# Attention and expert kernel: other PSUM banks for the second group's scores, finer last weight loads, two masks taken over by ScalarE and GpSimd

## What is computed

```python
q, k = exp(x @ Wq.T + bq), exp(x @ Wk.T + bk)        # per head, 16 heads of 8
v = x @ Wv.T + bv
kv = cumsum(k[..., None] * v[..., None, :], axis=1)   # over the tokens
den = sum(q * cumsum(k, axis=1), -1)
x1 = layernorm(x + (einsum(q, kv) / den) @ Wo.T + bo)
scores = sigmoid(x1 @ gate_w.T)                       # 32 experts, 2 of 4 groups, then top 8
w = 2.5 * chosen scores / their sum
moe = sum_e w_e * (silu(x1 @ gate_e.T) * (x1 @ up_e.T)) @ down_e.T  + the same, unweighted, of the shared expert
out = layernorm(x1 + moe)
```

## Time and profile before

| | us |
|---|---|
| median of 3 runs | 457.80 (457.75 to 458.01) |
| the profiled execution | 457.99 |
| its span (first to last instruction) | 456.2 |
| PE busy | 425.7 (93%) |
| DVE busy | 345.7 (76%) |
| POOL busy | 290.6 (64%) |
| ACT busy | 275.8 (60%) |
| DMA, mean | 99 GB/s |

### The profile page before, as it was taken

The page is one execution under the profiler, slowest core; times in us unless marked ns, Lnnn a source line. Parts: engine busy times, 40 slices in busy tenths (PEclk is TensorE's granted clock), DMA queues, the critical chain, the costliest instruction groups (busy, mean ns, idle before and its releaser), DMA issues.

```text
span 456.2 us, 10923 instructions
## 1 busy us (share of the span) xinstructions
PE 425.7 (93%) x4004; PEld 327.3 (72%) x4004; DVE 345.7 (76%) x912; ACT 275.8 (60%) x536; POOL 290.6 (64%) x217
## 2 busy tenths in 40 slices
PE   5888999999999999999999999999999999798992
PEld 3656787768776887868777787868877787476771
DVE  2648777896979877896968967796968968767653
ACT  3746357763696448763696448863697347445642
POOL 2555368745797368754797377755687467666781
PEclk9999999999999999999999999999999999999997
DMA  7500664145454453245463453245452443348300
GB/s 238 210 1 7 174 129 88 34 94 132 96 124 91 102 117 96 49 94 118 93 138 84 100 128 85 57 99 116 93 139 51 104 102 86 61 100 183 94 24 23
DMA packets 28677, 45.10 MB, mean 99 GB/s; under 512 B 2000, under 2 KB 10320, under 8 KB 28240
## 3 DMA queue, kind: packets, MB, share of 16 engines
q1 hardware_dynamic: 28624, 44.40, 40.9%
HBM read 41.77 MB, written 2.62 MB: 97 GB/s over the span
## 4 chain that ended last, share of the span: by engine, by line
PE 31%; DVE 29%; issue 13%; POOL 11%; ACT 5%; DMA 2%; DVEq 1%; ACTq 0%; SPq 0%; POOLq 0%
PE bank L345 30%; DVE units L955 7%; POOL units L1057 6%; DVE stats L801 2%; DVE hidden_lo L781 2%; DVE top_of_group L842 2%; POOL rstd L1076 2%; DVE bank L835 2%; POOL xT_lo L1083 2%; DVE x L813 2%; DMA weight_wide<-weight_d 1%; ACT v_pair L718 1%; ACT hidden_hi L637 1%; DVE replaced L874 1%; DVE out_sb L967 1%
## 5 line engine op out<-in xcount | busy, mean ns | idle before, releaser
L1057 POOL TENSOR_TENSOR units<-units,weight_wide 128x512 f32<-128x512 f32 x128 | 177.4, 1391 | 115.6 <-DVE units L955 106.7
L656 ACT ACTIVATE units<-bank 128x512 f32<-128x512 f32 x136 | 80.7, 594 | 74.0 <-PE bank L345 73.8
L781 DVE TENSOR_TENSOR hidden_lo<-units,hidden_hi 128x512 fp32r<-128x512 f32 x112 | 99.7, 892 | 23.3 <-ACT hidden_hi L637 23.3
L637 ACT ACTIVATE hidden_hi<-units 128x512 fp32r<-128x512 f32 x136 | 86.0, 633 | 51.1 <-POOL units L1057 49.4
L955 DVE TENSOR_TENSOR units<-bank,units 128x512 f32<-128x512 f32 x136 | 93.1, 685 | 29.8 <-PE bank L345 22.7
L345 PE MATMUL bank<-x_hi,gate_hi 128*128 128x512 f32 x136 | 62.1, 456 | 5.1 <-DVE units L955 4.8
L345 PE MATMUL bank<-x_hi,up_hi 128*128 128x512 f32 x136 | 54.5, 401 | 2.9 <-ACT units L656 2.9
L345 PE MATMUL bank<-hidden_hi,down_hi 128*128 128x512 f32 x136 | 54.9, 404 | 2.5 <-DVE hidden_lo L781 1.3
L345 PE MATMUL bank<-x_lo,gate_hi 128*128 128x512 f32 x136 | 54.1, 397 | 0.0
L345 PE MATMUL bank<-x_hi,gate_lo 128*128 128x512 f32 x136 | 53.9, 396 | 0.0
L345 PE MATMUL bank<-x_hi,up_lo 128*128 128x512 f32 x136 | 53.9, 396 | 0.0
(11 more groups left out here) (125 smaller groups left out, 689.2 us busy)
## 6 DMA issues: line engine op xcount, KB each, us to landing
weight_wide<-weight_d SPq DMA_DIRECT2D x62, 512.0 KB, 6.6
xT<-xT_in SPq DMA_DIRECT2D x8, 256.0 KB, 6.7
x_tok<-x_in SPq DMA_DIRECT2D x8, 256.0 KB, 7.0
out_dram<-out_sb SPq DMA_DIRECT2D x7, 256.0 KB, 2.3
weight_wide<-up_in SPq DMA_DIRECT2D x1, 1088.0 KB, 8.5
up_raw<-up_in SPq DMA_DIRECT2D x1, 1088.0 KB, 10.6
down_raw<-down_in SPq DMA_DIRECT2D x1, 1088.0 KB, 12.8
weight_d<-weightT SPq DMA_DIRECT2D x8, 64.0 KB, 1.6
```

The costliest lines, as they stand in the source:

```text
L637: nc.scalar.activation(hidden_hi[place(n, g)][:, :], units[place(n, g)][:, :], ACT.Copy).then_inc(hidden_hi_done, 1)
L656: nc.scalar.activation(units[place(n, g)][:, :], up_banks[2 * n % 3][:, :], ACT.Silu).then_inc(silu_done, 1)
L781: V.tensor_tensor(hidden_lo[place(n, g)][:, :], units[place(n, g)][:, :], hidden_hi[place(n, g)][:, :].bitcast(F32), ALU.subtract).then_in ...
L1057: G.tensor_tensor(units[place(n, g)][:, :], units[place(n, g)][:, :], weight_wide[:, w % (2 * PIECE), :], ALU.mult).then_inc(hidden_done, 1)
```

## The change

It has these parts:

1. **Start.** xT of group 0 and attn_cols are issued from ACT's queue, and have separate semaphores from attn_w. PE runs three matmuls of 256 columns on a zeroed tile (`unread`) before the weights are there. The bias matmul comes after the q projection, and DVE's addition of it after the prefix sums of k. The down weights are issued by SP after x_tok of group 1 and when the up weights have landed.
2. **Two masks of group 0.** The scores of the second sequence's quads 2 and 3 are copied by ACT into `probs` and multiplied by the triangle in place by POOL. ACT's gate_hi comes after den_cols and these copies, up_hi behind it. The late columns of gate_lo on POOL move from before to after x_lo of group 0.
3. **Second group's scores.** The first sequence's scores of group 1 are computed before block 2 of group 0 instead of after it; the denominator goes to `up_banks[0]`, the second sequence's first quad to `y_bank`, and the second sequence's scores run in two halves, each behind two masks. Block 3's `up` now waits for the denominator's copy, and the first `down` for the mask that reads `y_bank`. DVE's prefix sums of group 1 move ahead to just behind x1 of group 0, and the gate product of block 2 behind the first masks. hidden_hi and hidden_lo of block 0 move to slot 3. Six matmuls of `keep_warm` ("den" 3, "between" 2, and one of "up") go.
4. **Last group.** Piece 0 of its routing weights is loaded by `load_first` too (six transfers), and piece 1 is issued in slot 0, as soon as the group before has used up the buffer. Block 16's multiplication is done by DVE instead of POOL.

```diff
-WARM = {"x1": 6, "x1T": 2, "up": 1, "weight": 4, "den": 3, "between": 2}
+WARM = {"x1": 6, "x1T": 2, "up": 1, "weight": 4}
...
+            if m == 0:
+                return (mid_banks + up_banks + [y_bank] + mid_banks)[i]
+            first = y_bank if m == 1 and i == QUADS else o_bank
+            return ([first, work_bank] + mid_banks)[i % QUADS]
+
+        def den_bank(m):
+            return up_banks[0] if m == 1 else work_bank
...
         def ready_blocks(n, g):
             if g == 0 and n in (1, 2, 3):
-                return ((), (0,), (1, 2))[n - 1]
+                return (0, 1, 2) if n == 3 else ()
...
SP
+                    if f == 1:
+                        sp.wait_ge(up_loaded, 16)
+                        sp.sem_inc(apart, 1)
+                        sp.dma_start(down_raw, down_d).then_inc(down_loaded, 16)
...
-                    if m == 0:
-                        load_first()
+                    if m in (0, GROUPS - 1):
+                        load_first(m, 1 - u)
...
-                if ffn and n == 2:
+                if ffn and n == (2 if g < GROUPS - 1 else 0):
                     load_wide(1, g, u)
...
+                    sp.wait_ge(hidden_done, ROUTED * g - PIECE)
...
-                sp.wait_ge(hidden_done, reached(ROUTED * g + (1 if p == 1 else PIECE * (p - 1))))
+                sp.wait_ge(hidden_done, reached(ROUTED * g + (1 if p == 1 and g < GROUPS - 1 else PIECE * (p - 1))))
PE
-            pe.wait_ge(w_attn_loaded, 32)
-            pe.wait_ge(setup_chain, 1)
-            mm(mid_banks[0][:, 0:DIM], bv_wide[:, :], woT).then_inc(bias_mm, 1)
+            pe.wait_ge(setup_chain, 2)
+            for _ in range(3):
+                mm(y_bank[:, 0:256], unread[:, 0:128], unread[:, 128:384])
+            pe.wait_ge(w_attn_loaded, 16)
...
+                if g == 0 and n == 3:
+                    pe.wait_ge(den_copied, 2)
...
                 if mid and n == 0:
                     pe.wait_ge(qk_sum_done, reached(m + 1))
-                    if m == 1:
-                        keep_warm(WARM["den"])
                     if m == 0:
                         pe.wait_ge(kv_copied, SEQS)
+                    elif m == 1:
+                        pe.wait_ge(gated_done, 2)
...
+                    elif m == 1:
+                        for half in range(2):
+                            pe.wait_ge(probs_done, SEQS * QUADS + 2 * (half + 1))
+                            scores(m, 1, (2 * half, 2 * half + 1))
...
ACT
+            nc.scalar.dma_start(xT[:, :], xT_d[:, 0:GROUP]).then_inc(xT_loaded, 16)
+            nc.scalar.dma_start(attn_cols[:, :], attn_cols_d).then_inc(cols_loaded, 16)
...
-                if g == -2 and n == 16:
+                if m == 0 and mid and n == 1:
+                    for q in (2, 3):
+                        act.wait_ge(scores_ready, QUADS + q + 1)
+                        nc.scalar.activation(probs[:, 1, q, :, :, :].rearrange("p c j s -> p (c j s)"),
+                                             score_bank(0, QUADS + q)[:, :], ACT.Copy).then_inc(probs_copied, 1)
                     act.wait_ge(gate_loaded, 16)
                     nc.scalar.activation(gate_hi[:, :], gate_raw, ACT.Copy).then_inc(gate_split, 1)
...
DVE
+                if g == GROUPS - 1 and block_at(n, g) == ROUTED:
+                    dve.wait_ge(wide_loaded[PIECES - 1], loads_of(PIECES - 1, GROUPS))
+                    dve.wait_ge(gated_done, BLOCKS * g + n + 1)
+                    V.tensor_tensor(units[place(n, g)][:, :], units[place(n, g)][:, :],
+                                    weight_wide[:, 2 * PIECE - 1, :], ALU.mult).then_inc(last_hidden_done, 1)
-                if mid and n < 3:
+                if mid and n < 3 and not (m == 0 and n == 2):
                     masked_probs(m, 1 + n)
+                if m == 0 and mid and n == 2:
+                    dve.wait_ge(probs_masked, 2)
+                    dve.wait_ge(inv_turned, 2)
+                    dve.sem_inc(probs_done, 2)
...
POOL
+                    for q in (2, 3):
+                        pool.wait_ge(probs_copied, q - 1)
+                        own = probs[:, 1, q, :, :, :].rearrange("p c j s -> p (c j) s")
+                        G.tensor_tensor(own, own, tri.unsqueeze(1).to_broadcast([128, 2 * CHUNKS, CHUNK]), ALU.mult
+                                        ).then_inc(probs_masked, 1)
```

## The result

| | before | changed |
|---|---|---|
| median of four runs, us | 457.9 (457.75 to 458.41) | 452.89 (452.42 to 453.65) |
| ratio, with 95% interval | | 0.989 (0.9873 to 0.9907) |
| profiled execution, span | 457.99, 456.2 | 453.16, 451.4 |

What follows compares the result with a forecast made beforehand. PE was taken as the bound behind block 3 of group 0, with idle time at four places. Gains 1.3 + 0 + 2.8 + 1.9 + 0.6 = 6.6 us gave 451.4 profiled, 451.2 median; range 449.2 to 454.2.

Steps and rivals of the forecast that it cites:

- Start: From kernel start through the first projections: earlier xT and an earlier clock rise gain 1.3 us (0.4 to 2.3).
- The landing: At the start: xT, issued at 0.74, takes its own 3.5 us and lands at 4.24, gaining 1.0 us.
- The bias matmul: At the start: it moves behind q, 0.2 to 0.4 us of PE while ACT computes exp.
- The clock: At the start: three new matmuls may raise PE's clock one projection earlier; 0.3 us taken, up to about 0.9 possible.
- the start doesn't come earlier: Rival at the start: xT shares with attn_w and the clock rises as before; gain 0.2, total 452.3 us, chance 0.15.
- Group 0's attention: Group 0 up to attnT: sum 0, between 0.5 us lost and 0.3 gained, as ACT's order caps inv_denT at 22.3.
- Group 1's attention: Beside group 0's first blocks: block 3's up starts at 50.5 instead of 53.31, a gain of 2.8 us.
- the scores in halves: Group 1's second sequence: two halves of the scores cost 2.2 us, not 1.2.
- the rival with DVE or ACT as bound: Rival in group 1's attention: DVE or ACT limits the stage; gain 1.3 instead of 2.8, 452.7 us, chance 0.15.
- Last group: Last group's first blocks: small early loads start POOL 1.6 us earlier and bring the first down to 414.0, gaining 1.9.
- End: Last group's end: block 16's product on DVE takes about 0.68 us instead of POOL's 1.67, gaining 0.6 (0.3 to 0.9).
- Slower rival: Group 1's attention: without six keep-warm matmuls PE falls to 1.2 GHz; with six blocks 462 us, chance 0.02.

Runs made afterwards that it cites:

- c_late: The changed kernel with up_hi and down_hi later on ACT, four unread matmuls, and the bias matmul behind the transposes of k: 449.46 us, ratio 0.9815.
- c_held: The kernel c_late with up_raw issued only when gate_raw has landed, instead of right behind it: 450.60 us, ratio 0.9852.

## Why the prediction was right or wrong

**Start: wrong, -1.3 forecast, +0.29 measured.** Three steps of it failed. The landing: I gave xT its own 3.5 us, and it took 4.2, and attn_w, which I had left at 2.7, took 4.4. 0.22 of the 1.0 remained. The bias matmul, which I had hidden behind ACT's exp, stood in front of v and lay on the path with 0.45; -0.22 and +0.45 make most of the +0.29. The clock: I counted 0.3 as an addition, and it is the term that decides. Five profiles have this very start code, the changed kernel's and those with up_hi late, the banks undone, the last loads undone and the masks on DVE. In them the scores begin at 13.72, 11.56, 12.96, 13.14 and 11.34, so against the 13.43 of before the row lies anywhere from +0.29 to -2.09, by when the clock rose, and the changed kernel's profile is the worst of the five. Where the clock rose before the projections the row is -1.87 and -2.09, where it rose behind them it is -0.47, -0.29 and +0.29; the forecast's -1.3 lies between the two and is neither. The rival "the start doesn't come earlier" (0.2, 452.3) is what this profile shows, and a little worse.

**Group 0's attention: 0 forecast, -0.51 measured, outside its bound of 0.3.** ACT's order was the cap, as said; it let inv_denT start 8.63 behind the scores, where I had 8.87 (22.3 less 13.43). I called the 1.34 gap unexplained and left it; by its times it is PE waiting for its own instructions. The later down_raw is not the whole reason that it went: with down_raw early again the gap was 0.60, not 1.34, and the stretch 9.35 all the same. Not seen at all: that this cap is cheap to lift. Leaving the two masks on DVE gives 1.1 more (8.24), and up_hi behind inv_denT with the clock up and no gap 0.9 (8.44 in c_late).

**Group 1's attention: right, -2.8 forecast, -3.26 measured.** The mis-sized term is the scores in halves: 1.74 for both, not 2.2. DVE's slack of two blocks was enough; the rival with DVE or ACT as bound didn't occur. The 0.34 behind it need not be a loss of the change: this code took 35.53 to 36.04 in twelve profiles, the old order 35.56 and 35.54 in two.

**Last group: right in kind, -1.9 forecast, -1.19 measured.** POOL no longer waits for piece 0 and starts 1.54 earlier, as forecast (1.6). But its products run beside DVE's hidden_lo and take longer: the first two 2.86 us where they took 2.53 in the earlier trace rows, so the third starts 11.82 behind the write and not 11.39, and it takes 1.65 itself (408.61 to hidden_hi at 410.26), where I had taken 1.3. These two make up the missing 0.7. And the stall on piece 1 is not gone, as I had put it, but 1.41 us at 412.87; it delays no down. **End: -0.6 forecast, -0.44 measured**; DVE's product took 0.69, as taken.

**Slower rival.** It needed PE to idle in group 1's attention, where the six keep-warm matmuls went; there the only wait left is the 0.72 in front of 43.13. Two experiments show the price in small at other places, 1.6 us behind a wait of 1.57 and 0.9 behind one of 1.73. The Trainium skill (TensorE: Matmul & The Clock Gate, Part 1) says that throttled is the default state, and the traces agree: the granted clock reads 0.50 behind both waits. 0.02 for the case was low for a kernel with a wait of that length in group 0. The changed kernel's profile shows no such fall, and whether its slowest execution (453.65 us at 0.991) had one is open.

From write 1 to write 7 the kernel kept what came before, to 0.03 us in 311. The total, then, is right in its range partly by luck: the mechanism held for groups 1 and 7, while the start gave nothing and group 0 gave what wasn't counted.

## What to carry to other kernels

Where a kernel starts on a cold TensorE, moving operands forward is worth what the clock makes of it: four unread matmuls instead of three gave 1.5 us in the one pair of kernels that differ in nothing else, the second queue none in its pair. Look at the duration of a pass, not at the clock row, and at more than one profile, since the same start code differed by 2.4 us. Before an engine is relieved of work, see what the receiving engines have queued behind it: ACT's two copies of 1.1 us cost as much at attnT, while DVE, which was relieved, had the time. A gap of PE that nothing releases, inside a run of equal matmuls, may be its instruction fetch. Issuing a large load later that nobody needs yet shortened it here, but brought nothing while another engine capped the stage; and a load held so long that it lands after its first use costs (1.15 us from attnT to write 0 in c_held).

## What the runs showed of the hardware

- Two transfers of 256 and 272 KB issued at once from two queues landed in 3.7 to 4.8 us (twelve profiles); one behind the other from one queue, the first took 2.7 and 2.9, the second 3.5 and 4.0 (before, xT on SP).
- With three unread matmuls the rise of TensorE's clock came before the first projection in two profiles of eight, during the projections in one and behind them in five, as late as 10.7. The granted clock in the profile reads 1.00 in both cases, though passes take 1101 ns; a fall back later is shown there (0.50).
- PE stood still for 1.34, 1.00 and 0.60 us until 2.3 to 2.8 us behind the first packet of the queue of instructions, where it reached the place earlier than that, and not otherwise. That packet ran at 12.5 to 15.75 with down_raw late and at 17.0 to 17.75 with down_raw early. That PE's instructions are in it is inferred from these times.
- From write 1 to write 7 the same code took 310.5 to 310.6 us on one chip and 311.0 on two others; I have no cause for it.
